# Two-layer relational graph convolution on one core: root product behind four relations, table chunks spread over two products, keyed one-hots on VectorE

## What is computed

```python
def _rgcn_conv(x, src, dst, etype, W, root, b):
    seg = dst * num_rel + etype
    sums = segment_sum(x[src], seg, num_segments=num_nodes * num_rel)
    cnt = segment_sum(ones, seg, num_segments=num_nodes * num_rel)
    mean = (sums / max(cnt, 1)[:, None]).reshape(num_nodes, num_rel, -1)
    return einsum('nri,rio->no', mean, W) + x @ root + b

h = relu(_rgcn_conv(x, src, dst, edge_type, W1, root1, b1))
out = layernorm(x + _rgcn_conv(h, src, dst, edge_type, W2, root2, b2))
```

## Time and profile before

| | us |
|---|---|
| median of three runs | 1655.95 |
| the profiled execution | 1659.07 |
| its span, first to last instruction | 1657.3 |
| TensorE busy | 1523.6 |
| VectorE busy | 1127.0 |
| GpSimd busy | 759.4 |
| ScalarE busy | 673.1 |

### The profile page before, as it was taken

How to read it: one execution, slowest core, us unless ns; L and a number is a source line. 1 busy time by engine, 2 the same in 40 slices (tenths; PEclk the granted TensorE clock), 3 DMA queues, 4 the chain that set the end, 5 groups by cost and what they waited for, 6 DMA issues and landing times.

```text
span 1657.3 us, 24418 instructions
## 1 busy us (share of the span) xinstructions
PE 1523.6 (92%) x9003; PEld 1494.0 (90%) x9003; DVE 1127.0 (68%) x1705; ACT 673.1 (41%) x935; POOL 759.4 (46%) x547
## 2 busy tenths in 40 slices
PE   5999857899999999999896999799999999999996
PEld 5999857899899999999896999799999999898896
DVE  6789999436886565988894211565655656588696
ACT  3222323113544354676363012344443545366541
POOL 1111766404774454876650012545353635377470
PEclk9999978999999999999998999899999999999998
DMA  5353201213765555676543223555464646567552
GB/s 166 121 175 120 69 14 39 64 58 110 220 212 181 178 184 174 208 243 201 179 137 139 67 87 141 188 176 187 161 199 162 206 160 213 169 206 220 159 154 93
DMA packets 109222, 254.42 MB, mean 154 GB/s; under 512 B 18375, under 2 KB 81526, under 8 KB 109062
## 3 DMA queue, kind: packets, MB, share of 16 engines
q0 software_dynamic: 38400, 136.49, 27.4%
q1 hardware_dynamic: 70726, 116.65, 20.8%
HBM read 243.77 MB, written 65.45 MB: 187 GB/s over the span
## 4 chain that ended last, share of the span: by engine, by line
PE 54%; DVE 22%; issue 11%; DMA 8%; POOL 3%; ACT 1%; SPq 0%; ACTq 0%; DVEq 0%; POOLq 0%
PE prod L684 40%; PE agg L712 11%; DVE slot_hot L1121 5%; DVE g_low L934 4%; DMA raw<-y,bucket_index 3%; DMA y<-y_stage 3%; DMA x_rows<-in_x 2%; DVE g_high L934 2%; DVE ranks L1103 2%; POOL raw L429 2%; DVE ranks L1098 2%; DVE edge_f L1106 2%; DVE acc L941 2%; PE agg L822 2%; DVE dst_hot L1116 1%
## 5 line engine op out<-in xcount | busy, mean ns | idle before, releaser
L429 POOL DMA_INDIRECT raw<-y,bucket_index x480 | 621.4, 1295 | 515.7 <-DVE g_low L934 294.6
L684 PE MATMUL prod<-w_high,h_high 128*128 128x384 f32 x2160 | 733.3, 340 | 23.6 <-DVE acc L917 11.6
L684 PE MATMUL prod<-w_low,h_high 128*128 128x384 f32 x2160 | 727.8, 337 | 0.0
L684 PE MATMUL prod<-w_high,h_low 128*128 128x384 f32 x2160 | 726.5, 336 | 0.0
L934 DVE TENSOR_TENSOR g_low<-raw,g_high 128x768 fp32r<-128x768 f32 x320 | 293.4, 954 | 265.1 <-ACT g_high L540 222.4
L540 ACT ACTIVATE g_high<-raw 128x768 fp32r<-128x768 f32 x480 | 377.9, 839 | 143.9 <-DMA raw<-y,bucket_index 70.1
L684 PEld LDWEIGHTS prod<-w_high,h_high 128*128 128x128 f32 x2160 | 410.1, 190 | 26.3 <-issue 20.6
L684 PEld LDWEIGHTS prod<-w_low,h_high 128*128 128x128 f32 x2160 | 410.0, 190 | 0.0
L684 PEld LDWEIGHTS prod<-w_high,h_low 128*128 128x128 f32 x2160 | 409.3, 190 | 0.0
L573 ACT ACTIVATE y_stage<-prod 128x384 f32<-128x384 f32 x280 | 137.6, 491 | 616.9 <-PE prod L684 561.7
L712 PE MATMUL agg<-g_high,one_hot 128*128 128x384 f32 x960 | 253.2, 345 | 33.6 <-DVE g_low L934 23.4
(11 more groups left out here) (109 smaller groups left out, 654.8 us busy)
## 6 DMA issues: line engine op xcount, KB each, us to landing
y<-y_stage SPq DMA_DIRECT2D x280, 187.5 KB
w_raw<-in_w_all SPq DMA_DIRECT2D x36, 1152.0 KB
raw<-y,bucket_index POOLq DMA_INDIRECT x480
x_rows<-in_x SPq DMA_DIRECT2D x20, 375.0 KB
y<-in_x SPq DMA_DIRECT2D x1, 3750.0 KB, 15.1
y<-acc SPq DMA_DIRECT2D x10, 375.0 KB
out<-acc SPq DMA_DIRECT2D x10, 375.0 KB
bias<-in_b SPq DMA_DIRECT2D x2, 384.0 KB, 10.7
```

Of the source, the lines that this page charges most:

```text
L429: pool.indirect_dma_start(raw[:, slot_of, :], None, y[0:written * N, :], bass.IndirectOffsetOnAxis(ap=bucket_index[:, r * RT + i:r * RT + ...
L684: mm = pe.matmul(prod[:, bank, 0:HALF], left[:, k, t * P:(t + 1) * P], right[:, h, k, :], start=(k == 0 and left is h_high and right is w_ ...
```

## The change

- `ROOT1` becomes 4: relation 4 is now product 3 and the root product 4. The loads need no exchange of two matrices any more.
- The table's chunks stand behind two of every three steps, one chunk each, from product 2 step 9 to product 3 step 13 (`TABLE_AT`, `chunks_at`).
- `keyed` is made by VectorE, between `dst_hot` and `slot_hot`. GpSimd instead makes `w_low` of units 1 to 8 (`NEAR` is 9).
- The root's steps 10 to 19 carry the bucket sums of relation 1 (`second_half`). Product 5 carries relations 2 and 3, product 6 relation 4 as before.

```diff
-    ROOT1 = 3
-    TABLE_STEP = 8
+    ROOT1 = R // 2
+    TABLE_AT = 2 * STEPS + 8
...
-    NEAR = 7
+    NEAR = 9
...
+        def second_half(s):
+            return [("sum", 0, 1, s - T)] if s >= T else []
+
+        def chunks_at(step):
+            n = step - TABLE_AT
+            return range(n * 2 // 3, min((n + 1) * 2 // 3, CHUNKS)) if n >= 0 else range(0)
...
-                m = {ROOT1: ROOT1 + 1, ROOT1 + 1: ROOT1}.get(q, q) if isinstance(q, int) else q
-                w = w_all[bass.ds(m, 1), :, h * HALF:(h + 1) * HALF].rearrange("o (k p) n -> p (o k) n", p=P)
+                w = w_all[bass.ds(q, 1), :, h * HALF:(h + 1) * HALF].rearrange("o (k p) n -> p (o k) n", p=P)
...
-            def keyed_chunk(c):
-
-                if c >= 2:
-                    pool.wait_ge(chunk_counted, c - 1)
-                keys = is_key[:, :, c * CJ:(c + 1) * CJ].rearrange("p k j -> p j k")
-                for n, what in enumerate((SRC_UP, DL_UP)):
-                    ins = pool.tensor_tensor(keyed[:, c % 2, :, n * NB:(n + 1) * NB], keys,
-                                             edge_f[:, what, c * CJ:(c + 1) * CJ].unsqueeze(2).to_broadcast([EP, CJ, NB]),
-                                             ALU.mult)
-                ins.then_inc(keyed_ready, 1)
-
-            for u in range(1, 6):
+            for u in range(1, NEAR):
                 low_of_unit(u // 2, u % 2)
-            pool.wait_ge(keys_made, 1)
-            for c in range(CHUNKS):
-                keyed_chunk(c)
-                if c == CHUNKS // 2:
-                    low_of_unit(3, 0)
...
+            def table_keys(q):
+
+                def after(s):
+                    step = q * STEPS + s
+                    if step == TABLE_AT:
+                        act.wait_ge(keys_made, 1)
+                    for c in chunks_at(step + 1):
+                        copy_keys(c)
+                return after
...
-            matrix(2, 2, banks(0), after=table_keys)
-            high_of_unit(ROOT1, 1)
-            high_of_unit(ROOT1 + 1, 0)
-            matrix(4, 3, banks(0), two_relations(0, 1))
-            matrix(5, 4, banks(0), one_relation(2, None))
+            matrix(2, 2, banks(0), after=table_keys(2))
+            matrix(3, 3, banks(0), after=table_keys(3))
+            matrix(ROOT1, None, None, second_half)
+            matrix(5, 4, banks(0), two_relations(1, 2))
...
-                pe.wait_ge(keyed_ready, c + 1)
...
-            matrix(2, banks(0), staged(2), after=table_chunks)
+            matrix(2, banks(0), staged(2), after=table_chunks(2))
+            matrix(3, banks(0), staged(3), after=table_chunks(3))
...
                 if s == 3:
                     sum_flags()
+                if s >= T:
+                    bucket(0, s - T)
             pe.wait_ge(root_kept, STEPS)
-            matrix(4, banks(0), staged(3), two_relations(0, 1))
-            matrix(5, banks(0), staged(4), one_relation(2, None))
+            matrix(5, banks(0), staged(4), two_relations(1, 2))
...
+                keys = is_key[:, :, c * CJ:(c + 1) * CJ].rearrange("p k j -> p j k")
+                for n, what in enumerate((src_up, dl_up)):
+                    dve.tensor_tensor(keyed[:, c % 2, :, n * NB:(n + 1) * NB], keys,
+                                      what[:, c * CJ:(c + 1) * CJ].unsqueeze(2).to_broadcast([EP, CJ, NB]), ALU.mult)
...
-            for s in range(STEPS):
+
+            def keep_root1(s):
+                if s == 1:
+                    dve.wait_ge(w_low_ready, NEAR)
                 keep(STEPS * ROOT1 + s, s % T, s // T, s % BANKS, plus="bias")
-                if s == 2:
-                    low_of_unit(unit(ROOT1, 1))
-                if s == 12:
-                    low_of_unit(unit(ROOT1 + 1, 0))
-
-
+
+            matrix(ROOT1, second_half, keep_root1)
             in_parts = ((4, 0, K // 2), (7, K // 2, K), (13, 0, K // 2), (16, K // 2, K))
-            matrix(4, two_relations(0, 1), low_at=in_parts)
-            matrix(5, one_relation(2, 3), low_at=in_parts)
+            matrix(5, two_relations(1, 2), low_at=in_parts)
```

More of the change, by code:

```diff
@@ L70, in rgcn_residual_layernorm @@
     CHUNKS = EJ // CJ
-    ROOT1 = 3
-    TABLE_STEP = 8
-    assert N < 2048 and TABLE_STEP + (CHUNKS + 1) // 2 < STEPS
+    ROOT1 = R // 2
+    TABLE_AT = 2 * STEPS + 8
+    assert N < 2048 and TABLE_AT + CHUNKS * 3 // 2 + 1 < ROOT1 * STEPS
     MEAN1 = R
@@ L188, in rgcn_residual_layernorm @@
         keys_made = sem("keys_made")
-        keyed_ready = sem("keyed_ready")
         key_copied = sem("key_copied")
@@ L284, in rgcn_residual_layernorm @@
         block = ctx.enter_context(nc.Block())
-        TILE, DL, TYPE, SRC, KEY, ROW, GID, FLAG, RANK, SPOS, DL_UP, SRC_UP = range(12)
         @block.sync
@@ L826, in table_chunk, with table_chunks, after @@
                 mm.then_inc(chunk_counted, 1)
-            def table_chunks(s):
-                if s >= TABLE_STEP:
-                    for c in range(2 * (s - TABLE_STEP), min(2 * (s - TABLE_STEP + 1), CHUNKS)):
+            def table_chunks(q):
+                def after(s):
+                    for c in chunks_at(q * STEPS + s):
                         table_chunk(c)
+                return after
             def matrix(q, bank, free, actions=lambda s: [], spilled=None, middle=None, after=None):
@@ L980, in matrix @@
                             if keep_step:
-                                dve.wait_ge(root_kept, STEPS * (1 if q == MEAN1 else 3) + (s if q == MEAN1 else a[2]) + 1)
+                                dve.wait_ge(root_kept, {ROOT1: 0, MEAN1: STEPS, MEAN2: 3 * STEPS}[q]
+                                            + (a[2] if q == MEAN2 else s) + 1)
                             add(*a)
```

## The result

| | us |
|---|---|
| changed kernel, median of four runs | 1619.15 (1612.45 to 1620.9) |
| kernel before, same comparison | 1655.85 (1654.24 to 1659.86) |
| ratio | 0.9764, 95% interval 0.9736 to 0.9792 |
| profiled execution after, and its span | 1620.82, 1619.0 |

What follows compares the result with a forecast made beforehand. TensorE, busy 92% of the span, was taken to bound the kernel, held up in the table by GpSimd through VectorE. 52.0 us gained less 5.1 lost made 46.9, so a median of 1609 us, range 1601 to 1624.

Steps and rivals of the forecast that it cites:

- Where the time is lost: Table stretch, product 2 steps 8 to 16: 125.6 us taken where TensorE would need 69.6, so 56.0 us lost.
- Who causes it: In the table, TensorE waits 39.8 us for VectorE's `slot_hot`, which stands still while GpSimd operations run.
- Point 1: VectorE makes `keyed` in the table, two per chunk at 1.6 us each, so a chunk takes it 6.9 us.
- Both bounds: Price of one `keyed` on VectorE: 0.87 us from contiguous `dst_hot`, 1.98 us from GpSimd's median for the strided access.
- Point 2: Chunks spread two per three steps: TensorE needs 14.2 us, VectorE 13.8; 4 of 56 us remain lost, 52.0 gained.
- the first rival: In the table, `keyed` costs 1.98 us, a chunk 7.7; up to 15 us less gain, about 1619 us; chance 0.12.
- The ScalarE term of 2.8 us: At product 2 step 11 and product 3 step 1, `w_high` ahead of `key_hot` delays the copy 1.4 us each.
- The prediction's own sign of being wrong: Wrong if TensorE still waits for `hot_ready` in the table, `keyed` exceeds 2 us, or thirty sums lose over 20 us.
- Point 3: Root product moved behind product 3: the 4.4 us wait after `sum_flags` and 1.8 us more stay, change 0.
- Point 4: Ten sums of relation 1 in the root's second half: 2.6 us lost at step 10, 2.5 through `w_low`, 5.1 in all.
- Point 5: Product 5 takes two relations and takes over old product 4's loss (106.2 us against 97.0, 9.2 lost): change 0.
- From product 6 on: From product 6 to the end, both kernels do the same work in the same order: change 0.

## Why the prediction came out as it did

By its own steps, in the profiled spans (46.9 us forecast, 38.3 found):

- **Where the time is lost** was right: the table, with TensorE behind VectorE. *Who causes it* was right only as a row. That a `slot_hot` stands still while GpSimd works is so, but "the table is held up by GpSimd's operations" is not the whole cause: freeing VectorE of them and giving it the work gained 0.2%.
- **Point 1** failed by size. `keyed` was priced at 1.6 us from the strided reduction (one input, float32, so 680 bytes apart where `keyed` reads 340) and took 1.80, so a chunk is 7.3 us and not 6.9. Both bounds held (0.87, 1.98). The argument against the upper one, that ScalarE and GpSimd are slower on contiguous rows as well, holds for GpSimd (5.05 against 2.55 us for a `w_low`), but not for ScalarE (0.84 us for 768 elements, where VectorE's `g_low` of 768 takes 0.95).
- **Point 2** is the step that failed: "TensorE sets the pace, with these small losses". The holds by GpSimd were put at 1.2 us and the table at 126.6; the table took 135.3, and these 8.7 us are nearly the whole of the miss. About 2 of them are TensorE's own: a step behind a chunk takes 3.24 us and not 3.12, 17 times, so that three steps and two chunks need 14.48 us and not 14.2, and the table 124.7 us without any wait and not 122.6. The rest, but for 0.7 us, is waiting (6.9 us for `slot_hot`, 1.4 for `key_hot`) and the chunk at the lower clock (1.6), 9.9 us where 4 were forecast.
 The holds lengthened VectorE's work by 14.4 us. Each was set against 3.6 to 4.9 us to spare, as if the time to spare were whole each time. It was for the first hold, which cost TensorE 0.32 us (1.7 us in the run with ScalarE's copies first, which has no 1.39 us wait ahead of it). Then two chunks took VectorE 14.56 us against 14.48, and nothing was made up: VectorE ended chunk 7 at 240.76, and TensorE began it at 240.90. The second hold was paid with 4.74 us of waiting, and the third with 1.81. Even at 6.9 us a chunk the prediction's own numbers (13.8 against 14.2) would give back only some 1.3 us over the six chunks between two holds, by my estimate. This is the first rival, "VectorE paces the table", which said 1619 us at a price of 1.98. The contiguous source left 11.0 us of work in 14.48, and gave 9.8 us back.
 The ScalarE term of 2.8 us was in the sum too: one of its two waits appeared (1.39 us), and removing it changed nothing. The prediction's own sign of being wrong, that TensorE still waits for `hot_ready` in the table, was there.
- **Point 3** was right: 4.40 us of waiting and 2.4 of slower matmuls (4.4 and 1.8 forecast). Putting the flags earlier brought 6.8 us.
- **Point 4** was right within 1.1 us: root steps 10 to 19 took 54.7 us against 48.5, 6.2 lost for 5.1. The start was put at 2.6, and preparing ahead brought 2.5. The other piece was the whole `w_low`, 2.5 us on a VectorE whose cycle is already full. No run takes it away, but the traces fit: between root step 10 and the last kept step VectorE is idle for 1.2 us only (waiting for `g_high`), and halving the `w_low` gave 0.5 us, as is to be expected where two halves cost VectorE as much as the whole. Moving it ahead of step 10 was not tried.
- **Point 5** was right: product 5 took 107.0 us as product 4 had taken 106.2.
- **From product 6 on** 0 was forecast; the spans differ by 3.5 us there in favour of the change, and by 1.6 the other way ahead of the table. Product 2 step 8 begins anywhere from 181.5 to 183.3 us in the traces of the changed kernel and its variants, and runs of one kernel differ by more (1612.45 to 1620.9), so I give it no cause.

The clock followed the waits: 0.99 in the table, with one stretch at the lower level behind the 4.74 us wait, where none was forecast, and 1.00 in the two runs where that wait was gone (`w_low` on VectorE, contiguous `keyed`).

## What to carry to other kernels

When an engine stands still because of a neighbour, compare what the hold costs it with what the neighbour's work would cost it. GpSimd's `keyed` for two chunks cost VectorE 6.7 us (9.09 against 2.37 in the earlier trace rows), and making them costs 7.2: nothing was won. A `w_low` of GpSimd cost it 4.8 us, and making it costs 2.56: the kernel became faster. When a producer is to run beside a consumer, its work per period must leave room for the longest disturbance, and for making up that time before the next one: with 14.56 us in a period of 14.48 the holds were paid for, with 11.0 they were hidden. A price taken from another strided operation was 0.2 us too low here (1.6 for 1.80), so carry the sum at the upper bound as well, and ask first whether a contiguous copy of the same data lies there already.

## What the runs showed of the hardware

- The two-input product of 800 elements on VectorE takes 0.90 us from start to start from a contiguous bf16 source and 1.80 us from one with elements 340 bytes apart.
- `w_low` on GpSimd (5.05 us in the earlier trace rows) adds 4.8 us to ten `slot_hot` on VectorE (7.16 against 2.37), and 4.7 to 4.8 us to two `keyed` (8.36 and 8.49 against 3.67). It takes 5.56 to 5.78 us itself beside `slot_hot`, and beside `keyed` it took 9.43, 9.26 and 5.45 us. On VectorE the same `w_low` takes 2.56 us.
